# Graph attention over 4096 nodes: units of 1024 rows by 512 columns, sums of 129 columns, and bytes made on ScalarE

## The reference, cut to what matters

```python
# x: (4096, 128) f32, adj: (4096, 4096) int32, about 0.2% ones; W: (128, 128), a: (256, 1)
h = relu(layernorm(x))
Wh = h @ W
e = (Wh @ a1)[:, None] + (Wh @ a2)[None, :]
e = where(e > 0, e, 0.2 * e)
e = where(adj > 0, e, -9e15)
out = x + elu(softmax(e, axis=1) @ Wh)
```

## Time and profile before

| | |
|---|---|
| median of 3 runs | 271.23 us (268.96 to 271.58) |
| span of the profiled execution | 270.6 us |
| PE, PEld busy | 231.0, 213.2 us |
| DVE, ACT, POOL busy | 219.3, 151.7, 148.7 us |
| moved by DMA | 71.62 MB |

### The profile page before, as it was taken

How to read it: one execution, slowest core, us unless ns; L and a number is a source line. 1 busy time by engine, 2 the same in 40 slices (tenths; PEclk the granted TensorE clock), 3 DMA queues, 4 the chain that set the end, 5 groups by cost and what they waited for, 6 DMA issues and landing times.

```text
span 270.6 us, 7004 instructions
## 1 busy us (share of the span) xinstructions
PE 231.0 (85%) x2740; PEld 213.2 (79%) x2740; DVE 219.3 (81%) x430; ACT 151.7 (56%) x154; POOL 148.7 (55%) x89
## 2 busy tenths in 40 slices
PE   0067268349999999999999999999999999999991
PEld 0057257338999999999999999999999999999990
DVE  3597983572888898889889888988898889789885
ACT  0145336769994349537951994298349537951002
POOL 1469969423462993299049807950993299042002
PEclk9999875958999999999999999999999999999997
DMA  5999500079999956995899499949986995000101
GB/s 148 411 409 409 203 0 2 4 307 367 408 400 411 406 224 228 416 409 226 344 409 409 143 416 410 406 148 417 409 323 235 412 410 220 0 0 1 39 0 41
DMA packets 18921, 71.62 MB, mean 265 GB/s; under 512 B 736, under 2 KB 992, under 8 KB 18912
## 3 DMA queue, kind: packets, MB, share of 16 engines
q1 hardware_dynamic: 17760, 69.41, 65.5%
q10 hardware_dynamic: 1152, 2.10, 2.0%
HBM read 69.40 MB, written 2.10 MB: 264 GB/s over the span
## 4 chain that ended last, share of the span: by engine, by line
PE 79%; DVE 8%; POOL 3%; ACT 3%; DMA 3%; issue 3%; SPq 0%; POOLq 0%; ACTq 0%; DVEq 0%
PE acc L798 41%; PE acc L800 21%; PE mask_t L766 12%; DMA x_sb<-in_x_dram 3%; PE acc L730 2%; DVE val L539 2%; POOL rstd L298 2%; PE acc L741 2%; ACT mask L396 1%; DVE gq_hi L534 1%; PE acc L792 1%; POOL hn L305 1%; DVE gq_word L536 1%; ACT g_row L388 1%; DVE v L549 1%
## 5 line engine op out<-in xcount | busy, mean ns | idle before, releaser
L588 DVE SCALAR_TENSOR_TENSOR words<-g_row,gq_word,mask_t 128x512 f32<-128x512 uint8 (+1 forms) x256 | 172.6, 742 | 31.4 <-PE acc L800 27.8
L798 PE MATMUL acc<-val,words 128*128 128x258 f16 x1024 | 177.5, 274 | 0.0
L800 PE MATMUL acc<-val,words 128*128 128x129 f16 x1024 | 174.4, 219 | 0.0
L798 PEld LDWEIGHTS acc<-val,words 128*128 128x128 f16 x1024 | 99.7, 97 | 13.1
L314 POOL TENSOR_SCALAR mask<-raw 128x1024 uint8<-128x1024 int32 (+1 forms) x32 | 93.2, 2933 | 15.5 <-DMA raw<-in_adj_dram 15.5
L800 PEld LDWEIGHTS acc<-val,words 128*128 128x128 f16 x1024 | 100.0, 98 | 0.4
L396 ACT ACTIVATE mask<-raw,step_bias 128x3072 uint8<-128x3072 int32 (+1 forms) x32 | 87.2, 2795 | 0.1
L766 PE MATMUL mask_t<-ident_b,mask 128*128 128x128 bf16 x528 | 36.4, 224 | 6.5 <-ACT mask L396 6.5
L330 POOL TENSOR_TENSOR num<-acc_sb 128x516 f32<-128x516 f32 x7 | 7.7, 1104 | 59.8 <-ACT acc_sb L438 59.8
L766 PEld LDWEIGHTS mask_t<-ident_b,mask 128*128 128x128 bf16 x528 | 32.6, 115 | 7.5 <-issue 7.1
L396 ACT ACT_TABLE_LOAD x8 | 10.3, 1283 | 35.1 <-issue 34.8
(11 more groups left out here) (71 smaller groups left out, 139.6 us busy)
## 6 DMA issues: line engine op xcount, KB each, us to landing
raw<-in_adj_dram SPq DMA_DIRECT2D x32, 2048.0 KB, 12.3
x_sb<-in_x_dram SPq DMA_DIRECT2D x4, 512.0 KB, 8.0
out_dram<-x_sb ACTq DMA_DIRECT2D x8, 256.0 KB, 3.3
a_row<-in_L_gnn_a_dram SPq DMA_DIRECT2D x1, 128.0 KB, 6.7
w_sb<-in_L_gnn_W_dram SPq DMA_DIRECT2D x1, 64.0 KB, 3.2
```

Source lines behind the costliest of these rows:

```text
L588: nc.vector.scalar_tensor_tensor(words[:, q // HALF, q % HALF, :], g_row[:, bass.ds(c * CHUNK, CHUNK)], gq_word[:, 1, k:k + 1], maskt_byte ...
L798: nc.tensor.matmul(acc[:, t, 0:2 * V], high, val[:, tile].rearrange("p e v -> p (e v)"), start=False, stop=False, skip_group_check=True)
L800: last = nc.tensor.matmul(acc[:, t, 0:V], low, val[:, tile, 0], start=False, stop=False, skip_group_check=True)
```

## The change

- **Units.** A chunk has 1024 rows (8 row tiles, `CT`), a unit 512 columns (4 tiles, `BT`); 4 chunks of 8 units, again 32. `raw` and `mask` keep four slots of the same bytes; each unit's `raw` comes in two DMAs of 1 MB (512 rows each), in runs of 2 KB.
- **Products.** Each row tile and column tile has three matmuls of 129 columns. Three row tiles share a PSUM bank (three banks hold eight), and word tiles are 128x1024, four of them, each freed on its own.
- **Bytes.** ACT makes all of them, with `Sign` and a bias of -0.5, in two instructions of 128x2048 a unit; DVE makes the very first half. POOL makes none.
- **Seed.** The matmuls that opened each bank go. `seed_row` is made once, from the sum of the projected rows (POOL, then one PE matmul), and DVE adds it when it takes the sums out of the banks (`take_sums`, after the third word of the next chunk); ACT's copies of the banks and POOL's addition of the two halves go.
- **Preparation.** x comes in eight blocks of 256 KB. Rows are centred only, and the inverse deviation is multiplied in when the projection is taken out of PSUM (`keep_projected`). Bytes of units 0 and 1 are made among it. Only group 0 is made into values, words and a row before the products; for groups 1 to 3 this is done in chunk 0, by POOL (`weigh`), ACT and PE between the products. The weights `w` and `a` are loaded from ACT's queue, and `W a` is a matmul. PE runs matmuls that nobody reads (`keep_awake`).
- **End.** In the last unit PE finishes the first word for all tiles and then the rest tile by tile; sums are taken bank by bank, and relu and exp are done by ACT with the reciprocal as a scale; the result is stored in four pieces by SP.

The diff, cut to its core:

```diff
-GT = 8
-GROUP = GT * P
-CT = 4
+BT = 4
+BLOCK = BT * P
+CT = 2 * BT
...
+    adj_v = adj.rearrange("(c b p q) (u j) -> c b u p q j", b=2, p=P, q=BT, j=BLOCK)
...
+        def acc_tile(t):
+            return acc[:, t // PT, (t % PT) * V:(t % PT + 1) * V]
+        def acc_bank(k):
+            t0, t1 = BANKS[k]
+            return acc[:, k, 0:(t1 - t0) * V].rearrange("p (t v) -> p t v", v=V)
...
+            def load_x(b):
+                sp.dma_start(x_sb[:, b * BT:(b + 1) * BT, :], x_v[b]).then_inc(x_in[b], 16)
+            def load_raw(n, k):
+                sp.dma_start(raw[:, n % RING, k * BT:(k + 1) * BT], adj_v[n // U, k, n % U]).then_inc(raw_in[n % RING][k], 16)
+            for b in range(4):
+                load_x(b)
+            load_raw(0, 0)
+            for b in range(4, 6):
+                load_x(b)
+            load_raw(0, 1)
+            for b in range(6, NB):
+                load_x(b)
+            for n in range(1, C * U):
+                for k in range(2):
+                    if n == RING and k == 0:
+                        sp.wait_ge(first_bytes, 1)
+                    elif n >= RING:
+                        sp.wait_ge(act_bytes, 2 * (n - RING) + k)
+                    load_raw(n, k)
...
+            def weigh(g):
+                pool.wait_ge(z_ready, 2)
+                if g == 2:
+                    pool.wait_ge(vl_first, 2)
+                if g == 3:
+                    pool.wait_ge(vl_ready, 1)
+                nc.gpsimd.tensor_tensor(v32[:, g % 2], wh_sb[:, group(g), 0:F],
+                                        dv[:, group(g)].unsqueeze(2).broadcast_to([P, CT, F]), ALU.mult).then_inc(v32_ready, 1)
+                pool.wait_ge(vh_ready, g + 2)
+                nc.gpsimd.tensor_tensor(val[:, group(g), 1, 0:F], v32[:, g % 2], val[:, group(g), 0, 0:F], ALU.subtract
+                                        ).then_inc(vl_ready, 1)
...
+            def to_bytes(c, u, k):
+                n = c * U + u
+                act.wait_ge(raw_in[u % RING][k], (2 * c + u // RING + 1) * 16)
+                if n >= RING:
+                    act.wait_ge(turned, n - RING + 1)
+                nc.scalar.activation(mask[:, u % RING, k * BT:(k + 1) * BT], raw[:, u % RING, k * BT:(k + 1) * BT], ACT.Sign,
+                                     scale=1.0, bias=step_bias[:, 0:1]).then_inc(act_bytes, 1)
...
+            centre(0)
+            centre(1)
+            act.wait_ge(wt_ps, 1)
+            nc.scalar.copy(wa_t[:], aux[:, 0:W2]).then_inc(wt_ready, 1)
+            rectify(0)
+            act.wait_ge(wa_ps, 1)
+            nc.scalar.copy(w_sb[:, F:W2], aux[:, F:W2]).then_inc(wa_ready, 1)
+            rectify(1)
+            centre(2)
+            centre(3)
+            exponentials(0, 1)
+            rectify(2)
+            rectify(3)
+            row_copy(0, 0)
+            row_copy(0, 1)
+            high_values(0, 0, BT)
+            to_bytes(0, 0, 1)
+            centre(4)
+            centre(5)
+            rectify(4)
+            rectify(5)
+            high_values(0, BT, CT)
+            centre(6)
+            centre(7)
+            to_bytes(0, 1, 0)
+            rectify(6)
+            rectify(7)
+            to_bytes(0, 1, 1)
+            exponentials(1, G)
+            to_bytes(0, 2, 0)
+            to_bytes(0, 2, 1)
+            high_values(1, 0, CT)
+            to_bytes(0, 3, 0)
+            high_values(2, 0, CT)
+            to_bytes(0, 3, 1)
+            high_values(3, 0, CT)
+            for i in range(2 * (G - 1)):
+                row_copy(1 + i // 2, i % 2)
+                to_bytes(0, 4 + i // 2, i % 2)
+            to_bytes(0, 7, 0)
+            to_bytes(0, 7, 1)
+            act.wait_ge(vh_ready, 2 + G - 1)
+            for g in range(G):
+                square(g)
...
+            def keep_projected(g, k):
+
+                t0, t1 = BANKS[k]
+                tt = slice(g * CT + t0, g * CT + t1)
+                dve.wait_ge(wh_ps, 3 * g + k + 1)
+                dve.wait_ge(rstd_ready, g + 2 if g else 1 + (t1 > BT))
+                nc.vector.tensor_tensor(wh_sb[:, tt], projected(acc[:, k, :], t1 - t0),
+                                        half_rstd[:, tt].unsqueeze(2).broadcast_to([P, t1 - t0, W2]), ALU.mult).then_inc(wh_ready, 1)
...
+            def weights(c, u, q):
+                n = c * U + u
+                if q % 2 == 0:
                     if q == 0:
+                        dve.wait_ge(turned, n + 1)
+                if n >= 1:
+                    dve.wait_ge(words_free, 4 * n + q - WORDS + 1)
+                t = u * BT + q
+                nc.vector.scalar_tensor_tensor(words[:, q], g_row[:, c * CHUNK:(c + 1) * CHUNK], gq_word[:, 1, t:t + 1],
+                                               maskt_bytes[:, u % 2, q // 2, :, q % 2], ALU.max, ALU.mult).then_inc(words_ready, 1)
+            def take_sums(c):
+                dve.wait_ge(hp_ready, c + 1)
+                for k, (t0, t1) in enumerate(BANKS):
+                    wait_bank(dve, c, k)
+                    nc.vector.tensor_tensor(num[:, t0:t1], acc_bank(k), seed_row[:].unsqueeze(1).broadcast_to([P, t1 - t0, V]), ALU.add
+                                            ).then_inc(acc_free, 1)
+                dve.wait_ge(acc_free, 3 * c + 3)
                 nc.vector.reciprocal(rz[:], num[:, :, F]).then_inc(rz_ready, 1)
...
+            for b in range(2):
+                link(row_halves(b))
+                moments(b, b * BT, (b + 1) * BT)
+                centre(b)
+            row_halves(2)
+            link(row_halves(3))
+            moments(2, CT, 2 * CT)
+            for k in range(3):
+                keep_projected(0, k)
+            dve.wait_ge(raw_in[0][0], 16)
+            nc.vector.tensor_scalar(mask[:, 0, 0:BT], raw[:, 0, 0:BT], 0, None, ALU.is_gt).then_inc(first_bytes, 1)
+            make_words(0, 1, 3)
+            first_values(0)
+            split_weights_sums(0, 1, 3)
+            row_halves(4)
+            link(row_halves(5))
+            moments(3, 2 * CT, 3 * CT)
+            first_low_values(0)
+            first_values(1)
+            for k in range(3):
+                keep_projected(1, k)
+            row_halves(6)
+            link(row_halves(7))
+            moments(4, 3 * CT, 4 * CT)
+            first_low_values(1)
+            for k in range(3):
+                keep_projected(2, k)
+            dve.wait_ge(grow_ready, 2)
+            weights(0, 0, 0)
+            weights(0, 0, 1)
+            for k in range(3):
+                keep_projected(3, k)
+            weights(0, 0, 2)
+            weights(0, 0, 3)
+            for u in range(1, U):
+                for q in range(BT):
+                    if (u, q) == (1, 2):
+                        make_words(1, G, 6)
+                        split_weights_sums(1, G, 6)
+                        dve.wait_ge(word_ready, 4)
+                    if (u, q) == (7, 2):
+                        dve.wait_ge(mean_ps, 1)
+                        dve.wait_ge(consts, 6)
+                        nc.vector.tensor_scalar(seed_row[:, 0:F], aux[:, 0:F], SEED / N, None, ALU.mult).then_inc(mean_ready, 1)
+                    weights(0, u, q)
+            dve.wait_ge(mean_ready, 1)
+            for c in range(1, C):
+                dve.wait_ge(grow_ready, 2 * c + 2)
+                for u in range(U):
+                    for q in range(BT):
+                        weights(c, u, q)
+                        if (u, q) == (0, 2):
+                            take_sums(c - 1)
...
+            def product(c, u, q):
+                n = c * U + u
+                first = (u, q) == (0, 0)
+                pe.wait_ge(words_ready, 4 * n + q + 1)
+                tile = u * BT + q
+                for t in range(CT):
+                    if first and t % PT == 0:
+                        if c == 0:
+                            pe.wait_ge(wh_ready, 3 * (G - 1) + t // PT + 1)
+                        else:
+                            pe.wait_ge(acc_free, 3 * (c - 1) + t // PT + 1)
+                    high = words_h[:, q, t * P:(t + 1) * P, HI]
+                    low = words_h[:, q, t * P:(t + 1) * P, LO]
+                    nc.tensor.matmul(acc_tile(t), high, val[:, tile, 0, 0:V], start=first and t % PT == 0, stop=False, skip_group_check=True)
+                    nc.tensor.matmul(acc_tile(t), high, val[:, tile, 1, 0:V], start=False, stop=False, skip_group_check=True)
+                    last = nc.tensor.matmul(acc_tile(t), low, val[:, tile, 0, 0:V], start=False, stop=False, skip_group_check=True)
+                    if (u, q) == (U - 1, BT - 1) and t in (2, 5):
+                        last.then_inc(acc_done, 1)
+                last.then_inc(words_free, 1)
+            def last_product():
+                product(C - 1, U - 1, 0)
+                for t in range(CT):
+                    for q in range(1, BT):
+                        if t == 0:
+                            pe.wait_ge(words_ready, BT * (C * U - 1) + q + 1)
```

(20 more changed lines are left out.)

776 lines of the change are left out of this document (354 added, 422 removed).

## The result

| | before | changed kernel |
|---|---|---|
| time, median (lowest to highest), us | 270.57 (268.96 to 271.58) | 244.78 (244.50 to 244.87) |
| profiled execution: span, us | 270.6 | 243.0 |
| first product starts, us | 61.9 | 26.84 |
| last product starts, us | 264.5 | 235.1 |

The changed kernel takes 0.903 of the old time, 95% interval 0.897 to 0.909: 26 us less. The prediction was 249 us (242 to 260), so the sign and the range were right and the point 4 us too high. The time of a run is some 1.8 us above its span here (244.79 for the span of 243.0).

A forecast was written before the change was run, and what follows sets the result against it. PE was taken to bound the main loop, a chain of handovers the preparation. 31 + 2.3 + 201.6 + 2.9 + 4 + 6.8 gave a 248.6 us span; with the median 0.6 above it, 249 us, range 242 to 260.

The forecast's parts named there:

- first product, with 2.3 for the clock: Preparation: first product at 31 us, plus 2.3 us, half the 4.5 for three projections and a turn at low clock.
- 32 units of products, 31 turns: Main loop on PE: 3072 matmuls at 56.65 ns, 174.0 us, plus 31 turns, 27.6 us; 201.6 us in all.
- spreads and mean in chunk 0: PE work in chunk 0: six spreads of word rows at 0.45, 2.7 us, and the mean, 0.2 us.
- stalls: PE's waits in chunk 0: 0.4 for unit 2, 2.0 for unit 3's bytes, 1.5 for a spread; 4 us, 0 to 8.
- tail, from the last product: End of the kernel: last result, then a store of 2.4 us; 6.8 us, 0.7 more than before.
- the other signs: Trace marks of a right forecast: turns 6.3 us apart, words 1.2 us, ACT at 65-75% without loads between, DMA pauses.
- The rival of loads that don't hide: Main loop: 129-column matmuls don't hide their weight loads, 60 ns each, +10 us, 259 us; chance 0.06.
- the pole: Preparation after the first row copy at 17 us: ACT's steps, 12.2 us in sum, set the pace to 29.3 us.
- S: Start of the first product matmul, ending the preparation: 31 us, 28 below and 37 above; 33 with the clock's share.
- the spread (1,1): Chunk 0: this spread of word rows waits for ACT's row copy until 53.4, wanted at 51.9: 1.5 us stall.
- E + 4.4: Tail: time of the last result, 4.4 us after the last product's end E, before a store of 2.4 us.
- The rival: Transfers: 2 KB pieces at 250 GB/s put DMA's end at 297 us; decides from 302 GB/s down; chance 0.03.

The follow-up runs named there:

- extra_load: Changed kernel with a further unread 512 KB load behind each 1 MB load from chunk 1 on, 25 MB more: 278.26 us, ratio 1.029.
- no_keep: Changed kernel without the `keep_awake` matmuls that nobody reads: 245.94 us, ratio 0.908 to the kernel before.
- all_before: Changed kernel with words, rows and values of groups 1 to 3 all finished before the first product: 266.70 us, ratio 0.980 to the kernel before.
- pool_one: Kernel before, with one row tile instead of two converted by POOL in units 0 and 1: 264.07 us, ratio 0.975.
- pool_first: Changed kernel with the first half of unit 0's bytes (128x2048) made by POOL instead of DVE: 249.38 us, ratio 0.918 to the kernel before.
- two_seeds: Kernel before, with each of its 32 seed matmuls issued twice: 275.11 us beside 271.55, ratio 1.016.
- dve_scale: Changed kernel with the scaled values of groups 1 to 3 made by DVE instead of POOL: 242.83 us, ratio 0.895 to the kernel before.
- act_store: Changed kernel with the last of the four result stores issued by ACT instead of SP: 244.79 us, ratio 0.902 to the kernel before.
- both: Changed kernel with DVE scaling the values of groups 1 to 3 and ACT issuing the last store: 242.34 us, ratio 0.893 to the kernel before.

## Why the prediction was right, and where it was off

Each term of the sum beside the traces:

| term | predicted us | measured us |
|---|---|---|
| first product, with 2.3 for the clock | 33.3 | 26.84 |
| 32 units of products, 31 turns | 201.6 | 201.8 (32 x 6.333 - 0.89) |
| spreads and mean in chunk 0 | 2.9 | 2.9 (six of 0.44, 0.2) |
| stalls (what is left of 208.3 from first to last product) | 4 | 3.6 |
| tail, from the last product | 6.8 | 7.8 |
| span | 248.6 | 243.0 |

The mechanism was right, the start moved under chunk 0; the size of the start was not. The first product was expected at 31 to 35 us, with 28 as the lower bound, and came at 26.84. That the total still fell into the forecast's 243 to 256 owes something to luck: the longer tail and the time outside the span took back 2 us of the 6.5. Of the other signs, turns of 6.33 and words of 1.2 to 1.3 us held, ACT stood at 64% instead of 65 to 75, and DMA hardly paused before 191 us.

**The loop** was read rightly, by rows of another operation: the turn's 55.6 ns gave 56.65 for a 129-column matmul, and it takes 56.7. The rival of loads that don't hide (60 ns) is out: they take 98 ns each, as in the earlier trace rows (I had written 97), and hide. The Trainium skill (TensorE: Matmul & The Clock Gate, "Wait — 56ns, not 53.3ns?") states about 2.5 ns on top of the columns, which makes 56.25, an estimate; the measured 56.7, 2.9 ns above the columns, decides for the row.

**The first product** is the term that was mis-sized: 6.5 us too high, more than the whole sum (5.6). Its steps:
- To the first row copy I had 17; it starts at 13.61. The statistics began at 3.69 instead of 4.0, and a block took DVE 1.9 us (next statistics at 5.61 and 7.53) instead of 2.3; the last scaling ends at 11.36 instead of 12.7. The first bytes took 1.22 us instead of 2.3: no row of the kernel before had this form on DVE, and I had priced its 2048 elements at nearly twice what they take. The remaining 1.0 is the splits and the spread, each shorter than I had them.
- ACT was the pole, as predicted: 13.61 to 24.9, 11.3 us of the 12.2 summed.
- The 2.3 us for the clock were mostly not paid. The clock did fall (0.87 in 20 to 30, the projection at 20.14 took 3.21 and the turn at 18.81 1.54 instead of 0.89), but PE did this while ACT was the pole, so most of it was hidden; the last projection, on the path, ran in 2.05. I had charged a slower PE to the path without asking what covered it. `extra_load` prices it: its kernel is the same up to there, its clock read 1.00 from 10 to 30 us, and its first product came at 26.38. So the fall cost about 0.5 us. In both PE had stood idle for 1.9 us before 17.8; why the clock fell in one and not in the other is open; without the dummy matmuls (`no_keep`) it did not fall either.

**Where the gain comes from.** "Nearly all comes from S: 60 to 33" stands: `all_before` undoes the overlap and loses 22 of 26 us, 2 of them by the slow first products. But S is two causes. One is the overlap. The other is that POOL no longer holds DVE: the prediction named that stall and then gave it no price of its own. It was worth about 7 us in the kernel before (`pool_one`) and 4.6 in the changed one (`pool_first`). The parts are measured in different kernels and don't add up: `all_before` keeps the freed DVE and yet is only 5 us faster than the kernel before, less than the 7 of `pool_one`. Its other steps are thus slower in serial order, 2.2 us of it by the low clock at its first products; the rest was not traced to a step. The loop went from 204.5 to 201.8: the seeds gave 3.5 (`two_seeds`), the dummy turn 0.9, the start at low clock 1.4, and 1024 triples of 170 ns instead of pairs of 167 took back 3.1: 2.7 by parts, and 2.7 by the spacing of the turns.

**Stalls.** 3.6 us against 4, two of three as named. Expected were 0.4 for unit 2, 2.0 for unit 3's bytes and 1.5 for the spread (1,1); seen were none, 1.36 (44.19) and 1.3 (47.91), and 0.43 at 77.71. Measured from the start of one matmul to the next, less its spacing, the two are 1.5 each, which makes up the 3.6. They are the ones of the chain POOL, ACT, PE that I wrote down, smaller since POOL began at 34.08 instead of 39. The third I had not: ACT sums the values for the mean in four passes from 69.19 to 73.87, 4.7 us, which my account of ACT left out; "from there ACT gets ahead" was too quick. `dve_scale` shows that the chain was real: 1.3 us sooner from unit 4's turn on, and 2.0 in all.

**Tail.** Predicted E + 4.4 for the last result, measured 239.42, E + 4.2. What was short is the stretch behind it: 2.4 us as in the kernel before against 3.6. The last store is issued at 240.14, 0.7 us after its result, since SP issues four of them. That this alone sets the end fell with `act_store`: issued by two queues, the run ends at the same time. From the last result to the end of the span it is 3.6 us here, 3.8 in `act_store`, 3.0 in `dve_scale` and 2.7 in `both`. In each of them, and in the kernel before, the end comes 0.3 to 0.4 us after the last store issued has landed; from issue to landing it takes 2.5, 3.4, 1.8 and 2.2 us, and 2.0 before. So the landing sets the end, and why it varies is open.

**Transfers.** 2 KB reads of 16 KB rows came at 386 GB/s where the stream of 4 KB reads came at up to 412 in 62 to 75 us of the kernel before: 6% less. The earlier trace rows had said "no worse"; they could not tell, as the prediction granted. The rival stayed away since 386 is above both 302 and the 327 of `extra_load`. Runs and transfers both halved, so which of them costs the 6% is open. The threshold was wrong, though nothing came of it: the part outside the transfers is 30 us and not 20. Had the rate been 310 GB/s, the prediction would have called it safe, and transfers would have been the bound.

**Time and span.** The median stood 0.6 above the span of the profiled execution of before; where both are known of one execution, the time is 1.7 to 2.2 us above its span. So that profile was most likely of an execution 1 to 2 us longer than the median, and its 270.6 and my 0.6 do not belong together: 1.2 us too little for the changed kernel, hidden by the larger error.

## What to carry to other kernels

When the engines take turns before a saturated main loop, start the loop as soon as its first unit can run and move the rest of the preparation under it; here undoing it cost 22 of 26 us, while all that changed in the loop gave 2.7, the bigger word instruction 0.5 in chunk 0, and the tail grew by 1.7. A tiny DVE instruction that takes microseconds and ends together with a POOL instruction is a wait and not work: take it out first, and try a smaller POOL instruction, since here one constant in the old kernel gave about 7 us. To price a transfer bound, count what follows the last load in the order that the code issues it, not in the order in which the data depend.
